# A graph network on one core: edge sums behind a sorter get a second pair of banks, loads move, and the attention layer's VectorE steps are reordered

## What is computed

```
x = layernorm(x + mlp0(x + segsum(w * x[dst]) / segsum(w)))            # layer 1: weights by dst
x = layernorm(x + mlp1([x, segsum(ea64, dst), segmax(ea64, dst), mean, u]))   # layer 2
h = relu([x[src], x[dst]] @ W1 + b1); h = h @ W2 + b2
x = layernorm(x + segmean(h * sigmoid(h @ Wg + bg), src))               # layer 3: by src
g = leaky_relu(xl[src] + xr[dst] + ea16 @ W_e, 0.2)
logits = einsum(g, att)                                                 # layer 4: 4 heads of 16
ex = exp(logits - segmax(logits, dst)[dst])
out = segsum(xl[src] * ex / segsum(ex, dst)[dst], dst) ...; x = layernorm(x + gelu(batchnorm(out) + x))
```

## Time and profile before

| | |
|---|---|
| median of 3 runs | 6778.48 us |
| profiled execution | 6777.28 us |
| its span, first to last instruction | 6775.5 us |
| TensorE busy | 3900.6 us (58%) |
| VectorE busy | 3850.9 us (57%) |
| GpSimd busy | 3542.2 us (52%) |
| ScalarE busy | 1823.0 us (27%) |
| HBM traffic | 99 GB/s over the span |

### The profile page before, as it was taken

The page is one execution under the profiler, slowest core; times in us unless marked ns, Lnnn a source line. Parts: engine busy times, 40 slices in busy tenths (PEclk is TensorE's granted clock), DMA queues, the critical chain, the costliest instruction groups (busy, mean ns, idle before and its releaser), DMA issues. The chain is left out here.

```text
span 6775.5 us, 58450 instructions
## 1 busy us (share of the span) xinstructions
PE 3900.6 (58%) x12498; PEld 2265.4 (33%) x12498; DVE 3850.9 (57%) x4586; ACT 1823.0 (27%) x3467; POOL 3542.2 (52%) x3649
## 2 busy tenths in 40 slices
PE   3556544675444444444444435777778787777770
PEld 2344432454222222222222223333344344433340
DVE  9988844632333333333333343777787778777774
ACT  1233322342111111111111111333333333333330
POOL 5430032215666666666666656665666556565542
PEclk7666667765776676666676655666666656666665
DMA  5545577502343334333343312333333333333320
GB/s 157 166 155 165 163 164 197 181 8 59 95 102 100 102 99 103 98 102 98 101 103 98 100 40 58 81 84 75 82 86 84 80 80 86 80 81 78 81 69 22
DMA packets 1365705, 671.25 MB, mean 99 GB/s; under 512 B 1042970, under 2 KB 1246324, under 8 KB 1364706
## 3 DMA queue, kind: packets, MB, share of 16 engines
q1 hardware_dynamic: 1090118, 338.26, 21.0%
q0 software_dynamic: 116096, 120.71, 9.5%
q10 hardware_dynamic: 159390, 211.24, 8.9%
HBM read 344.19 MB, written 325.64 MB: 99 GB/s over the span
## 5 line engine op out<-in xcount | busy, mean ns | idle before, releaser
L1565 POOL DMA_INDIRECT got<-tabg,ix x1568 | 1479.0, 943 | 960.3 <-issue 426.0
L1373 POOL DMA_INDIRECT got<-tabg,ix x1568 | 1479.0, 943 | 830.8 <-issue 441.9
L1393 PE MATMUL p_inter<-hid,W 128*128 128x512 f32 x392 | 381.1, 1073 | 1251.9 <-DVE run L1479 983.9
L1471 DVE TENSOR_TENSOR_SCAN own<-mk,own,p_first 128x512 f32<-128x512 bf16 x195 | 248.8, 1276 | 1419.3 <-remote 806.0
L175 PEld LDWEIGHTS p_out<-ident,run 128*128 128x128 f32 (+1 forms) x3136 | 580.8, 219 | 577.7 <-issue 572.1
L175 PE MATMUL p_out<-ident,run 128*128 128x128 f32 (+1 forms) x3136 | 684.2, 372 | 64.5 <-issue 57.0
L490 DVE TENSOR_TENSOR_SCAN run<-p_mk,run,feat 128x512 f32<-128x512 f32 x390 | 477.2, 1265 | 243.2 <-ACT feat L583 84.1
L1393 PEld LDWEIGHTS p_inter<-hid,W 128*128 128x128 f32 x392 | 93.6, 297 | 1295.9 <-issue 1163.3
L1728 DVE TENSOR_TENSOR p_pre<-own,p_pre 128x512 f32<-128x512 f32 x196 | 136.0, 694 | 561.0 <-issue 313.5
L1617 PE MATMUL p_logit<-act_in,AT 128*128 128x512 f32 x392 | 288.7, 826 | 284.9 <-DVE act_in L1734 157.2
L558 PE MATMUL p_mk<-mk,sel 2*128 2x512 bf16 x392 | 166.5, 517 | 450.8 <-DVE run L490 367.3
(11 more groups left out here) (309 smaller groups left out, 7414.7 us busy)
## 6 DMA issues: line engine op xcount, KB each, us to landing
t<-rows ACTq DMA_DIRECT2D x195, 512.0 KB
first<-start SPq DMA_DIRECT2D x780, 128.0 KB
t<-rows ACTq DMA_DIRECT2D x195, 288.0 KB
got<-tabg,ix POOLq DMA_INDIRECT x3136
start<-zeros SPq DMA_DIRECT2D x100, 500.0 KB
ea<-in_ea_dram SPq DMA_DIRECT2D x390, 128.0 KB
mk<-marks SPq DMA_DIRECT2D x780, 64.0 KB
start<-zeros SPq DMA_DIRECT2D x195, 256.0 KB
```

Source lines behind the costliest of these rows:

```text
L1373: nc.gpsimd.indirect_dma_start(got[s][0:g.p, cc, h, :], None, tabg, bass.IndirectOffsetOnAxis(ap=ix[0:g.p, g.n, h, cc:cc + 1], axis=0)).th ...
L1393: nc.tensor.matmul(p_inter[s][:, 0:g.w], W2[:, :], hid[s][:, 0:g.w], start=True, stop=True).then_inc(mixed, 1)
L1471: nc.vector.tensor_tensor_scan(own[s][:, 0:g.w], mk[m][:, 0:g.w], p_first[s][:, 0:g.w], prime[:, 0:1] if g.zero else own[1 - s][:, W - 1:W ...
L1565: nc.gpsimd.indirect_dma_start(got[s][0:g.p, cc, h, :], None, tabg, bass.IndirectOffsetOnAxis(ap=ix[0:g.p, g.n, h, cc:cc + 1], axis=0)).th ...
```

## The change

Four edits.

1. In `sort_and_edge_sums`, from group 109 on (the tick after the last turn, `ALONE`), marks go alternately to `p_mk` and to the sorter's `p_keys`; TensorE waits for the scan of two groups before, and after the last turn it waits until ScalarE has emptied `p_keys`.
2. The zero fills go one for every group instead of every second, so they end at group 99. Of the index loads only the four of `src` stay in this stage, now at groups 8, 24, 40 and 56.
3. The four index loads of `dsts` move to the first `node_chain`, on SP's queue behind the weights, with a wait at the end of the stream.
4. In `edges_4`, VectorE's order becomes maximum, exponents, **spread (0), attend (1), denominators (2), leak (1), accumulate (2)**: `spread` goes ahead of `attend`, and the scan `den`, cut out of `accumulate`, ahead of `leak`. The maximum's scan takes its start value from the other buffer directly, and the copy of the column goes to ScalarE's `exps`.

```diff
+    ALONE = ticks_of_turns[-1] + 1
+        alone_banks = (p_keys, p_mk) if ALONE % 2 == 0 else (p_mk, p_keys)
-            run_ticks(eng, a, NG + 1 + max(lag for lag, _ in groups), groups)
+            run_ticks(eng, a, NG + 1 + max(lag for lag, _ in groups), alone)
...
-                    if behind > 10 and behind % 4 == 0 and index_rows:
+                    if n % 16 == 8 and index_rows:
                         to, rows_in = index_rows.pop(0)
                         sp.dma_start(to, rows_in).then_inc(indexed, 16)
-                    if n % 2 == 0 and len(filled) < 100:
+                    if len(filled) < 100:
                         blank.fill(sp, len(filled), len(filled) + 1)
-                sp.wait_ge(indexed, 16 * 8)
+                sp.wait_ge(indexed, 16 * 4)
...
# scan
+                    banks = alone_banks[g.n % 2] if g.n >= ALONE else p_mk
...
# tensor
+                def spread_and_turn_alone(g):
+                    turn_group(g)
+                    pe.wait_ge(maxed, g.n - 1)
+                    spread_marks(g, alone_banks[g.slot(2)])
+                    if t == len(turns_at) - 1:
+                        pe.wait_ge(back, 4 * len(turns_at))
...
# node_chain, SP
+                for to, index_rows in indices:
+                    sp.dma_start(to, index_rows).then_inc(indexed, 16)
...
+                wait_from(sp, indexed, 16 * len(indices))
...
# edges_4, scalar, exps
+                    nc.scalar.activation(top[1 - s][:, 0:1], top[s][:, W:1 + W], ACT.Copy).then_inc(carried, 1)
...
# edges_4, vector
-                        nc.vector.tensor_copy(top[s][:, 0:1], top[1 - s][:, W:W + 1]).then_inc(carried, 1)
-                    dve.wait_ge(carried, g.n + 1)
-                    nc.vector.tensor_tensor_scan(..., top[s][:, 0:1], ALU.add, ALU.max)
+                    nc.vector.tensor_tensor_scan(..., NEG if g.zero else top[1 - s][:, W:1 + W], ALU.add, ALU.max)
+                    wait_from(dve, carried, g.n)                      # in exponents, before L1709
-                each_group(dve, (2, maximum), (2, exponents), (1, attend), (0, spread), (1, leak), (2, accumulate))
+                each_group(dve, (2, maximum), (2, exponents), (0, spread), (1, attend), (2, denominators), (1, leak), (2, accumulate))
```

More of the change, by code:

```diff
@@ L230, in build @@
             marks_1 = Marks(nc, sb, ps, sem, c, 1, srcs, marks, ident)
[L231 removed]
+            sort_and_edge_sums(nc, sb, ps, sem, si, di, flip, srcs, dsts, ends, ends_1, marks_1, blank, src, ix4,
                                ea64, marks, t1, wsum, wn, ident, sel2)
[L233 removed]
+        node_chain(nc, sb, ps, sem, X, order[0], order[1], srcs, nid, ident, prime, t1, (w2a[D:2 * D, :], w2a[0:D, :]), None, tabg[0], start2, tuple(index_loads(dsts, ix3)),
                    (wn, w0a, b0a, w0b, b0b, u1, w1a, b1a, w1b, b1b, g1, be1))
@@ L377, in scans_beside, with sort_and_edge_sums @@
     return out
-def sort_and_edge_sums(nc, sb, ps, sem, si, di, flip, srcs, dsts, ends, ends_1, marks_1, blank, indices, ea64, marks, t1, wsum, wn, ident, sel2):
+def sort_and_edge_sums(nc, sb, ps, sem, si, di, flip, srcs, dsts, ends, ends_1, marks_1, blank, src, ix4, ea64, marks, t1, wsum, wn, ident, sel2):
     steps = list(network())
@@ L409, in sort_and_edge_sums, with between_turns @@
         scanned = (summed, maxed)
+        alone_banks = (p_keys, p_mk) if ALONE % 2 == 0 else (p_mk, p_keys)
         def keys_at(turn):
             return (kb, ka) if turns_at[turn] % 2 == 0 else (ka, kb)
-        def between_turns(eng, groups, turn):
+        def between_turns(eng, groups, turn, alone):
             a = 0
@@ L434, in load @@
                     sp.dma_start(mk[s][:, :, 0:g.w], marks[0][:, :, ds(row, g.w)]).then_inc(ea_in[s], 16)
-                index_rows = [pair for table, ix in indices for pair in index_loads(table, ix)]
+                index_rows = list(index_loads(src, ix4))
                 sp.wait_ge(blank.cleared, 1)
@@ L550, in _, with turn_group, spread_marks, spread_and_turn @@
             def _(pe):
-                def spread_and_turn(g):
-                    s, t = g.slot(AHEAD), g.slot(2)
+                def turn_group(g):
+                    s = g.slot(AHEAD)
                     pe.wait_ge(ea_in[s], 48 * g.turn(AHEAD) + 48)
                     wait_from(pe, feats, g.n - 1)
-                    turn_to_features(nc, p_in[t], ea[s], g, ident).then_inc(turned, 1)
-                    wait_from(pe, maxed, g.n)
-                    for kind in range(2):
-                        mm = nc.tensor.matmul(p_mk[kind][:, 0:g.w], sel2[:, :], mk[s][:, kind, 0:g.w], start=True, stop=True)
-                    mm.then_inc(spread, 1)
+                    turn_to_features(nc, p_in[g.slot(2)], ea[s], g, ident).then_inc(turned, 1)
+                def spread_marks(g, banks):
+                    for kind in range(2):
+                        mm = nc.tensor.matmul(banks[kind][:, 0:g.w], sel2[:, :], mk[g.slot(AHEAD)][:, kind, 0:g.w], start=True, stop=True)
+                    mm.then_inc(spread, 1)
+                def spread_and_turn(g):
+                    turn_group(g)
+                    wait_from(pe, maxed, g.n)
+                    spread_marks(g, p_mk)
+                def spread_and_turn_alone(g):
+                    turn_group(g)
+                    pe.wait_ge(maxed, g.n - 1)
+                    spread_marks(g, alone_banks[g.slot(2)])
                 def turn_back(g):
@@ L885, in bn, with node_chain @@
     return t.unsqueeze(2).to_broadcast((P, k, width))
-def node_chain(nc, sb, ps, sem, X, info, info_next, key, nid, ident, prime, source, weights, biases, tabg, start, mlp=None):
+def node_chain(nc, sb, ps, sem, X, info, info_next, key, nid, ident, prime, source, weights, biases, tabg, start, indices=(), mlp=None):
     width = 2 * D if mlp else D
@@ L906, in node_chain @@
         p_tab, p_prime = ps(c, "p_tab", [P, 4, 2 * D]), ps(c, "p_prime", [P, 1])
-        cleared, small_in, weights_in, chain, ready = (sem(c, n) for n in ("cleared", "small_in", "weights_in", "chain", "ready"))
+        cleared, small_in, weights_in, chain, ready, indexed = (sem(c, n) for n in ("cleared", "small_in", "weights_in", "chain", "ready", "indexed"))
         rows_in = [sem(c, f"rows_in{u}") for u in range(NU)]
```

20 lines of the change are left out of this document (12 added, 8 removed).

## The result

The changed kernel took 6859.69 us (median of 8 runs, 6833.6 to 6885.11); the kernel before, run beside it, 6781.81 (8 runs, 6775.63 to 6802.29). The ratio is 1.0109, with a 95% interval of 1.0085 to 1.0132: slower by about 1%, where 6515 us was forecast. The profiled execution took 6847.44 us, with a span of 6845.7.

What follows compares the result with a forecast made beforehand. Bound by a chain of stages behind barriers, the attention layer by TensorE's 8.27 plus VectorE's 4.28 us a group: 6777.3 - 196 (attention) - 75 (left-over groups) + 6 (sort) + 3 (node chain) = 6515 us, range 6390 to 6680.

Steps and rivals of the forecast that it cites:

- 14 x 9 = 126 us ... I leave them as they are: Attention layer: the excess of 14 long VectorE waits, 126 us, stays unchanged and enters no term of the sum.
- The halts: Attention layer: 14 waits of VectorE before the sum into p_pre, 165.9 us in all, their cause not in the rows.
- Rival D: Attention layer: a denser loop meets more halts, 9 us each; at one in three groups 6974 us; chance 0.05.
- 1.0 us a group: Attention layer: saving from VectorE's new order, taken between 0.84 and 1.25; 196 us for 196 groups.
- rival B: Attention layer: TensorE keeps 2.4 GHz, GpSimd's 10.0 us sets the pace; up to 360 us saved, 6350 us; chance 0.20.
- The argument against B: Attention layer: TensorE was busy 75% yet mostly at 1.2 GHz, so activity alone doesn't release the throttle.
- The floor: Attention layer: GpSimd's eight gathers take 10.0 us a group, below the 11.5 left, so they don't bite on the mean.
- The price of the column: Attention layer: moving the maximum's column copy from VectorE to ScalarE changes nothing on the path; zero.
- The left-over groups: Stage after the sort: alternate banks 28 us, index loads moved 40, fills gone 7; 75 us saved, from 20 to 135.
- The two holes: Left-over groups: two stretches of some 55 us, little moving while GpSimd issues 49 gathers; expected to stay.
- The node chain: First node chain: the four moved index loads cost +3 us, from 0 to +30.

Runs made afterwards that it cites:

- after_4: The changed kernel run once more without edits, on a chip without halts: 5663.42 us, 0.927 of the kernel before.
- before_again: The kernel before run once more without edits, on a chip without halts: 6123.04 us.
- pause_both: The changed kernel with GpSimd filling an unread tile (about 1.7 us) after each gather batch in both edge layers, chip with halts: 6591.5 us, 0.9621 of the kernel before.

## Why the prediction was wrong

**The step that failed** is "14 x 9 = 126 us ... I leave them as they are". The halts were taken for a fixed tax of 126 us, and the sum has nothing for new ones; but they follow the pace. The change made 26 more of them, +285 us. Rival D had the mechanism (a denser loop meets more of them, 29 more to break even) and got 0.05, because in the trace of before 14 in 196 looked rare. The 26 were fewer than 29, but the gain against them was 138 us in the layer and 76 before it, not 262, so they were enough for a loss of 71 us (70 by the profiled executions). Its price was near: 9 us each, where a long interval holds 8.2 us above an ordinary one before and 10.0 after.

What could have been read: D was set aside for want of a sign that quick ticks have more halts. The sign was in the trace of before, where all nine single batches that began soon after the gather ahead, and four of the five chains, hold one, and none of 159 others. And the forecast said that GpSimd's 10.0 us "don't bite on the mean". They need not. In the earlier trace rows GpSimd idles 960.3 us ahead of 1568 gathers; without the 426.0 between them ("issue") 534 are left, a pause of 2.7 us a group. Every microsecond off the group comes off that pause. The other edge layer, with the same ten microseconds of gathers a group, took 11.8, with 806.0 us of VectorE's idle time before it marked "remote", which nothing in the program explains.

**1.0 us a group** was mis-sized to the other side. Without halts it is 1.95, as rival B (0.20) had it: `own` and `den` fill the waits as described, and TensorE then ran mostly at 2.4 GHz, 0.79 of full clock against 0.64 (of the 392 matmuls of L1623, 294 took under 0.8 us in after_4, 132 in before_again). So the forecast was off there too, the other way: the whole gain is 444 us (6107.4 to 5663.4), not 262. In after_4 a quick group reads:

```profile
4503.28 1.27 DVE L1741 TENSOR_TENSOR_SCAN own<-mk,own,p_first 128x512 f32<-128x512 bf16 x1
4503.44 1.12 PE L1623 MATMUL p_pre<-theirs,ident 128*128 128x512 f32 x2
4504.68 0.69 DVE L1749 TENSOR_TENSOR p_pre<-own,p_pre 128x512 f32<-128x512 f32 x1
4505.28 1.27 DVE L1763 TENSOR_TENSOR_SCAN den<-decay,den,p_logit 128x512 f32<-128x512 f32 x1
4506.47 0.67 DVE L1755 TENSOR_TENSOR act_in<-p_pre,fifth 128x512 f32<-128x512 f32 x1
4507.05 0.69 DVE L1769 TENSOR_TENSOR p_logit<-theirs,p_logit 128x512 f32<-128x512 f32 x1
4507.65 0.74 DVE L1772 SCALAR_TENSOR_TENSOR mixed<-den,for_den,p_reset 128x512 f32<-128x512 f32 x1
```

From the sum to `mixed` 2.97 us, where 3.0 was forecast and 4.28 was before; the pair into p_pre takes 1.12 at the quick level, 2.08 in the earlier trace rows. 147 of its 195 intervals are under 10.5 us, 2 of before_again's. The argument against B, TensorE busy 75% and still slow, confused the slow clock's long instructions with work: at 0.64 the same instructions are 1875 us, at 0.79 1539.

**The floor** held, 195 x 10.0 = 1950. The price of the column (zero) couldn't be seen by itself.

**The left-over groups** were right: -72 to the last scan against -69, the first of the last 84 groups 3 us later (6 forecast), the median distance of the groups from there on 3.58 before and 2.90 after (2.75 forecast), with `p_keys` and `p_mk` in turn:

```profile
1172.89 2.46 DVE L493 TENSOR_TENSOR_SCAN run<-p_keys,run,feat 128x512 f32<-128x512 f32 x2 [0.44 <-ACT feat L599]
1175.30 2.46 DVE L493 TENSOR_TENSOR_SCAN run<-p_mk,run,feat 128x512 f32<-128x512 f32 x2
1178.52 2.46 DVE L493 TENSOR_TENSOR_SCAN run<-p_keys,run,feat 128x512 f32<-128x512 f32 x2 [0.76 <-ACT feat L599]
```

What is late next is ScalarE's `feat`, one of the three engines named. The two holes stayed on the chips with halts (of some 57 and 61 us) and are absent in after_4: they are halts as well, under 49 gathers in a row. The node chain is 4 us shorter, not 3 longer.

**Still open:** why some chips (or hours) make halts and by what path GpSimd's gathers hold up the others, whether gathers or rows count, whether 14 is typical of the kernel before, and what the best pause is on a chip with halts. Of the versions run that compute the whole result, pause_both is the fastest on such a chip (0.9621) and the changed kernel itself on one without (0.927).

## What to carry to other kernels

When all engines stall at once and one queue goes on, look at that queue first: compare its pauses in rounds with a stall and in rounds without, and ask what your change will do to them. When you speed up the consumers of a feeder, work out the feeder's pause per round, not only its busy time; the mean may leave room where a single round doesn't. And a time from one chip can have the wrong sign for another: here 1.01 on one sort and 0.93 on the other, told apart only by running the kernel before again.

## What the hardware showed

- The same program took 6781.8 to 6860.6 us on three jobs' chips and 6103.0 to 6107.4 on three others', 11 to 12% apart. The difference is where GpSimd gathers: the other edge layer 2300 against 1935 us, the layer of the change 2463 against 2332, the sort stage with its two times 49 gathers 1289 against 1181, the first node chain 343 against 304 (before and before_again).
- On the chips with halts, SP's register instructions go from 0.03 to 0.7 us and other engines' hand-overs arrive together, up to 13 us late, while GpSimd issues gathers with no pause or one under 2.6 us from start to start. Single instructions cost the same: an indirect gather of 128 rows 0.943 to 0.946 us on both, a 128x512 scan of the own rows 1.276. The granted clock in the layer was 0.64 on both for the kernel before; for the changed one it was 0.72 with halts and 0.79 without.
- TensorE's busy share did not tell its granted clock in the layer: 0.64 at 1875 of 2330 us busy and 0.79 at 1539 of 1950, 80% and 79%.
